# Two graph-attention layers on one core: scores, products and transposes of a tile in one run each

## The chip, the cores and the metric

The kernel runs on one core of a Trainium2 chip. The metric is device time of one execution in microseconds (us). Before the change it is 2035.97 us, the median of three runs (2034.86 to 2036.61). Differences within 0.2% (about 4 us) can't be told from no change for this kernel.

## The reference, cut to what matters

A graph of 3125 nodes with 128 features and 103,125 edges goes through a relational graph convolution with residual and normalization, and then through two attention layers with two heads of 64 features, the first followed by a relu, the second by a residual and a normalization:

```
def _transformer_conv(x, src, dst, Wq, bq, Wk, bk, Wv, bv, Ws, bs, heads):
    q = (x @ Wq + bq).reshape(n, heads, C)
    k = (x @ Wk + bk).reshape(n, heads, C)
    v = (x @ Wv + bv).reshape(n, heads, C)
    alpha = jnp.sum(q[dst] * k[src], axis=-1) / np.sqrt(C)
    amax = jax.ops.segment_max(alpha, dst, num_segments=n)
    ex = jnp.exp(alpha - amax[dst])
    denom = jax.ops.segment_sum(ex, dst, num_segments=n)
    a = ex / denom[dst]
    out = segment_sum(v[src] * a[..., None], dst).reshape(n, heads * C)
    return out + x @ Ws + bs
...
h = jax.nn.relu(_transformer_conv(x, ..., HEADS))
x = _layernorm(x + _transformer_conv(h, ..., HEADS), axis=-1)
```

All arithmetic is float32.

## The kernel before, in words

The first half of the kernel builds, among other things, a dense table `bias` of 3125 x 3125 values: the logarithm of how many edges lead from one node to another. With it the attention is done densely: for a tile of R = 125 target nodes all 3125 scores of each head are computed, the table is added, and nodes without an edge fall out in the softmax.

The function `conv` does one attention layer; it is called twice. It has T = 25 tiles. The 3125 source nodes are cut into CH = 7 chunks, six of 500 and one of 125. For a tile the work is:

- **Scores** (TensorE, L1499): for each chunk and each of the two heads one matmul of the keys `kT_l` with the queries `q_tile_l`. A head takes 64 of the 128 rows of the array, so that the two heads of a chunk can run side by side. 14 matmuls; the trace records two passes for each (float32), so 8 records are two chunks.
- **Masking** (VectorE, L1703): one operation for each chunk and head takes the scores out of their PSUM bank, adds the table and keeps the maximum. Then the row maximum is formed (L1734, L1738).
- **Exponentials** (ScalarE, L1600): four operations over a tile, two for each head.
- **Transposes** (TensorE, L1514): 50 transposes of 125x125 in 14 turns (a turn is a chunk of one head; the two short ones are turns 12 and 13). Each turn fills a PSUM bank, which ScalarE (L1608, L1610) or VectorE (L1711, turns 1, 4, 7, 10) copies to SBUF.
- **Products** (TensorE, L1485): 50 matmuls of the values with the transposed weights, each into 64 of the array's columns (two heads, two column halves); 100 records. All add up in bank `psO`.
- **Ending**: ScalarE copies the sums (L1591), TensorE transposes them and multiplies the tile by `Ws` (L1549, L1550), VectorE divides and adds (`finish`, L1654 to L1666). In layer 1 the rows are transposed once more for layer 2 (L1558, L1633). In layer 2 `center` and `normalize` (L1673 to L1685) add the residual and normalize, with a power on GpSimd (L1453) in between.

The order is written out by hand. A step t of the loop works on the scores of tile t, on the transposes and products of tile t - 1 (`u`), and on the ending of tile t - 2 (`w`). Every engine has its own `step`; counting semaphores join them. TensorE alternates: two chunks of scores, three turns, two chunks, three turns, two chunks, three turns, the short chunk, five turns, then all products. PSUM has eight banks: four hold scores (`psS`), three hold turns (`psT`), the last is `psO`.

Of the kernel before, what the change touches and what calls it, by code (L numbers as in the profile page):

```python
# [1332 lines left out]
def conv(nc, a, m, layer, out):  # L1333
# [4 lines left out]
    with ctx:  # L1338
# [3 lines left out]
        def sem(name):  # L1342
# [33 lines left out]
                 "rooted", "carried", "ot_ok", "o_ps", "x_cur", "q_laid", "kk_ps", "bq_ok")  # L1376
# [6 lines left out]
        psS, psT, psO = ps[0:4], ps[4:7], ps[7]  # L1383
        psQ = ps[4:8]
        ORDER = (0, 1, 2, 3, 4, 5, 6, 7, 8, 12, 13, 9, 10, 11)
        ON_V, ON_A = (1, 4, 7, 10), (0, 2, 3, 5, 6, 8, 12, 9, 11)
# [5 lines left out]
        def turned(u, i):  # L1392

            return u * NT + (ORDER.index(i) + 1)
# [13 lines left out]
        @block.sync  # L1408
        def _(sp):
            def step(t, par):  # L1410
                if inside(t):

                    if not is_int(t) or t >= 2:
                        sp.wait_ge(z["masked"], (t - 1) * NT)
                    sp.dma_start(bias[par][:, :], m["bias"][bass.ds(t, 1), :, :].rearrange("a p n -> (a p) n")).then_inc(b_in[par], 16)

                if layer == 2 and inside(t - 1):
                    if not is_int(t) or t >= 3:
                        sp.wait_ge(z["asked"], t - 2)
                    sp.dma_start(x_old[1 - par][:, 0, :], m["x1"][bass.ds((t - 1) * R, R), :]).then_inc(x_in[1 - par], 16)  # L1420
                if layer == 2 and inside(t - 3):
                    sp.wait_ge(z["rows_ok"], t - 2)
                    sp.dma_start(out[bass.ds((t - 3) * R, R), :], rows[1 - par][:, 0, :]).then_inc(out_ok[1 - par], 16)
            pipeline_loop(sp, step, 3)
            if layer == 2:
                sp.wait_ge(out_ok[0], 16 * ((T + 1) // 2))
                sp.wait_ge(out_ok[1], 16 * (T // 2))

        @block.gpsimd
        def _(pool):  # L1430
            nc.gpsimd.memset(half_power[:, :, :], -0.5).then_inc(z["one"], 1)
            pool.wait_ge(z["one"], 1)
            pool.wait_ge(z["q_ok"], 1)

            def lay_q(t, par):

                if not is_int(t) or t >= 2:
                    pool.wait_ge(z["qk"], (t - 1) * NT)
                nc.gpsimd.tensor_copy(q_now[par][:, :], qT[:, bass.ds(t * R, R)]).then_inc(z["q_laid"], 1)  # L1439

            lay_q(0, 0)
            pool.wait_ge(z["q_ok"], CH)

            def step(t, par):
                if inside(t + 1):
                    lay_q(t + 1, 1 - par)
                if inside(t - 2):
                    if not is_int(t) or t >= 4:
                        pool.wait_ge(z["o_ps"], t - 3)
                    nc.gpsimd.tensor_copy(x_now[par][:, :], inT[:, bass.ds((t - 2) * R, R)]).then_inc(z["x_cur"], 1)  # L1450
                if layer == 2 and inside(t - 2):
                    pool.wait_ge(z["asked"], t - 1)
                    nc.gpsimd.tensor_tensor(rstd[:, :, :], rstd[:, :, :], half_power[:, :, :], ALU.pow).then_inc(z["rooted"], 1)  # L1453
            pipeline_loop(pool, step)

        @block.tensor
        def _(pe):
# [31 lines left out]
            def scores(t, par, j):  # L1489
                if j == 0:  # L1490
                    pe.wait_ge(z["q_laid"], t + 1)
                if is_int(t) and t == 0:
                    pe.wait_ge(z["k_ok"], j + 1)

                if not is_int(t) or t * CH + j >= 2:
                    pe.wait_ge(z["masked"], (t * CH + (j - 2)) * 2 + 2)
                for hd in range(HEADS):
                    own = slice(HD * hd, HD * (hd + 1))
                    nc.tensor.matmul(psS[2 * ((par + j) % 2) + hd][0:R, 0:cw[j]], q_now[par][own, :],  # L1499
                                     kT[own, CW * j:CW * j + cw[j]], start=True, stop=True).then_inc(z["qk"], 1)  # L1500

            def turn(u, up, i):
                c, hd = i // HEADS, i % HEADS
                if c in (0, EXP_AT):
                    pe.wait_ge(z["exp_ok"], u * 4 + (hd + 1 + 2 * (c > 0)))

                if 3 <= i < 12:
                    chunk_out(pe, u, i - 3)
                elif i < 3 and (not is_int(u) or u >= 1):
                    chunk_out(pe, u - 1, i + 9)  # L1510
                for b in range(cw[c] // R):
                    n = 4 * c + b
                    to = psT[i % 3][0:R, b * R:(b + 1) * R] if c < CH - 1 else psO[0:R, 128 * (hd + 1):128 * (hd + 1) + R]
                    last = nc.tensor.transpose(to, S[up][:, hd, n * R:(n + 1) * R], eye[0:R, 0:R])  # L1514
                last.then_inc(z["t_ps"], 1)
# [18 lines left out]
            def step(t, par):  # L1534
# [7 lines left out]
                if is_int(t) and t == 1:  # L1542
                    pe.wait_ge(z["v_ok"], len(groups))
# [7 lines left out]
                if inside(t):  # L1551
                    scores(t, par, 2)
                    scores(t, par, 3)
                if inside(u):
                    turns(u, up, 3, 6)
# [3 lines left out]
                if inside(t):  # L1559
                    scores(t, par, 4)  # L1560
                    scores(t, par, 5)
                if inside(u):
                    turns(u, up, 6, 9)
                if inside(t):
                    scores(t, par, 6)
                if inside(w):
                    pe.wait_ge(z["fin_ok"] if layer == 2 else z["r_ok"], w + 1)
                if inside(u):
# [8 lines left out]
        def _(act):  # L1577
# [25 lines left out]
            def turned_out(u, i):  # L1603
# [3 lines left out]
                if c < CH - 1:  # L1607
                    nc.scalar.copy(PT[i][:, 0:cw[c]], psT[i % 3][0:R, 0:cw[c]]).then_inc(z["pa_ok"], 1)  # L1608
                else:
                    nc.scalar.copy(PT[i][:, 0:256].rearrange("p (h n) -> p h n", h=HEADS)[:, :, 0:R],  # L1610
                                   psO[0:R, 128:384].rearrange("p (h n) -> p h n", h=HEADS)[:, :, 0:R]).then_inc(z["pa_ok"], 1)

            def step(t, par):
                u, up, w = t - 1, 1 - par, t - 2
                if inside(u):
                    for i in (0, 2, 3, 5):
                        turned_out(u, i)
                if layer == 1 and inside(w):
                    rows_turned(w, par)
                if inside(u):  # L1620
                    for i in (6, 8, 12, 9, 11):
                        turned_out(u, i)
                if inside(t):
                    for n in range(3):
                        exps(t, par, n)
                if inside(u):
                    sums_out(u, up)
                if inside(t):
                    exps(t, par, 3)
# [7 lines left out]
        def _(v):  # L1637
# [49 lines left out]
            CHAIN = 2 if layer == 1 else 6  # L1687

            def step(t, par):
# [7 lines left out]
                def mask(j):  # L1697
                    v.wait_ge(z["carried"], t * CH + j) if not is_int(t) or t * CH + j > 0 else None
                    v.wait_ge(z["qk"], (t * CH + (j + 1)) * 2)
                    V.memset(spare[:, :], 0.0).then_inc(z["carried"], 1)  # L1700
                    for hd in range(HEADS):
                        lo, hi = CW * j, CW * j + cw[j]
                        V.tensor_tensor_reduce(S[par][:, hd, lo:hi], psS[2 * ((par + j) % 2) + hd][0:R, 0:cw[j]],  # L1703
# [3 lines left out]
                def turned_out(i):  # L1707
# [3 lines left out]
                    V.tensor_copy(PT[i][:, 0:cw[c]], psT[i % 3][0:R, 0:cw[c]]).then_inc(z["pt"], 1)  # L1711

                if inside(t):
                    mask(0)
                    mask(1)
                if inside(u):
                    turned_out(1)
                if inside(w):
                    finish(w, par, then)
                if inside(t):  # L1720
                    mask(2)
                    mask(3)
                if inside(u):
                    turned_out(4)
                if inside(t):
                    mask(4)
                    mask(5)
                if inside(u):
                    turned_out(7)
# [9 lines left out]
                if is_int(t) and t == 0:  # L1739
                    values_out()  # L1740
                if inside(u):
                    turned_out(10)
                if layer == 2 and inside(w):
                    center(w, par, then)
                    normalize(w, par)
            pipeline_loop(v, step)
# [21 lines left out]
```

## Time and profile before

| | |
|---|---|
| Median of three runs | 2035.97 us |
| The profiled execution | 2030.42 us, span 2028.5 us |
| TensorE matmul busy | 1952.3 us, 96% of the span |
| TensorE weight loads busy | 1633.2 us, 81% |
| VectorE busy | 1431.0 us, 71% |
| ScalarE busy | 1297.1 us, 64% |
| Mean granted TensorE clock | 0.986 |
| Attention, layer 1 (first projection to next layer's) | 1066.79 to 1547.72 us |
| Attention, layer 2 (first projection to the end) | 1547.72 to 2028.5 us |

The span is from the first to the last instruction; the time of an execution is a little more. Ends of matmuls are modelled in the trace and they overlap in the array, so what TensorE really spends on a group is read from the start of one row to the start of the next, not from the row's length. The two attention layers are about half of the time, each some 481 us, and nearly all of it is 24 like steps.

### The profile page before, as it was taken

To read this page: it belongs to the slowest core of one execution; us is meant where nothing else is said; L and a number is where in the kernel's file an instruction comes from. 1 tells how busy PE (TensorE), PEld (TensorE's weight loads), DVE (VectorE), ACT (ScalarE), POOL (GpSimd) and SP (SyncE) were. 2 spreads that over 40 slices of the span, in tenths; PEclk is the share of its full clock that TensorE was granted. 3 is DMA by queue.
4 is the path that set the end of the run, shared out by engine and by line. 5 is a ranking of instruction groups with operands and counts; after the bars stand their busy time and mean duration, and the time that the engine had idled before them with its cause. 6 is when DMAs were issued, how large, how long until landed. Compare 5 with 4: busy or idle time off the path is not lost. (4 is left out here: it accounts for less than half of the span.)

```text
span 2028.5 us, 53132 instructions
## 1 busy us (share of the span) xinstructions
PE 1952.3 (96%) x19165; PEld 1633.2 (81%) x19165; DVE 1431.0 (71%) x4127; ACT 1297.1 (64%) x2289; POOL 671.6 (33%) x802
## 2 busy tenths in 40 slices
PE   1799999999999999999989999999999999999998
PEld 1789999999999999999975777777776777777777
DVE  3888878878887887888635666666663766677665
ACT  1566766767676676767645666666664666666665
POOL 3676577566657656665210000000000000000000
PEclk8899999999999999999999999999999999999999
DMA  3012111111211111121013222222211233222220
GB/s 80 9 38 76 42 40 52 65 39 39 77 40 40 53 64 39 39 78 37 34 67 128 96 69 90 95 95 84 73 63 71 94 104 103 84 87 101 102 102 8
DMA packets 43018, 137.00 MB, mean 68 GB/s; under 512 B 9190, under 2 KB 24359, under 8 KB 36484
## 3 DMA queue, kind: packets, MB, share of 16 engines
q1 hardware_dynamic: 38484, 128.24, 17.7%
q0 software_dynamic: 4400, 6.80, 1.4%
q8 instruction: 104, 1.70, 0.4%
q14 instruction: 30, 0.25, 0.0%
HBM read 91.83 MB, written 43.20 MB: 67 GB/s over the span
## 5 line engine op out<-in xcount | busy, mean ns | idle before, releaser
L854 PE MATMUL ps<-matrixT,x_rows 125*128 125x256 f32 (+1 forms) x2500 | 563.5, 377 | 0.1
L1703 DVE CUSTOM_DVE_ANT_0 scores_l<-ps,bias_rows_l 125x500 f32<-125x500 f32 (+1 forms) x700 | 396.6, 619 | 212.5 <-issue 212.5
L854 PEld LDWEIGHTS ps<-matrixT,x_rows 125*128 125x128 f32 x2500 | 461.3, 190 | 48.4 <-issue 0.2
L1608 ACT COPY weightsT_l<-ps 125x500 f32<-125x500 f32 x400 | 230.4, 577 | 293.4 <-PE ps L1514 292.8
L945 ACT COPY matrixT<-ps 125x500 f32<-125x500 f32 (+2 forms) x800 | 381.9, 652 | 44.3 <-PE ps L842 44.3
L1514 PEld LDWEIGHTS ps<-eye,scores_l 125*125 125x125 f32 x2500 | 287.8, 188 | 114.5 <-issue 106.7
L842 PE MATMUL ps<-high_weights,low_onehot 64*125 64x125 f32 x6300 | 368.2, 275 | 11.1 <-DVE high_weights L722 11.1
L842 PEld LDWEIGHTS ps<-high_weights,low_onehot 64*125 64x125 f32 x6300 | 357.9, 189 | 24.7 <-issue 15.8
L1514 PE MATMUL ps<-eye,scores_l 125*125 125x125 f32 x2500 | 324.9, 280 | 1.3 <-ACT weightsT_l L1608 1.3
L1600 ACT ACTIVATE scores_l<-scores_l,neg_max_l 125x1500 f32<-125x1500 f32 x200 | 318.0, 1594 | 7.5 <-DVE neg_max_l L1738 7.5
L1499 PE MATMUL ps<-kT_l,q_tile_l 64*125 64x500 f32 (+1 forms) x1400 | 317.0, 564 | 1.5 <-DVE chunk_max_l L1703 1.2
L719 DVE TENSOR_TENSOR low_onehot<-own_low,digitsT 128x1000 f32<-128x1000 f32 x200 | 281.4, 1407 | 0.0
L1485 PE MATMUL ps<-weightsT_l,values_l 125*64 125x125 f32 x5000 | 279.7, 271 | 0.0
L1485 PEld LDWEIGHTS ps<-weightsT_l,values_l 125*64 125x64 f32 x5000 | 267.8, 136 | 5.9
L722 DVE TENSOR_TENSOR high_weights<-high_weights,edge_weightsT 128x800 f32<-128x800 f32 x200 | 222.7, 1114 | 0.0
L1499 PEld LDWEIGHTS ps<-kT_l,q_tile_l 64*125 64x125 f32 x1400 | 114.7, 182 | 103.9 <-issue 63.0
L574 POOL TENSOR_TENSOR coef_parts<-kinds,comp 128x512 f32<-128x512 f32 x97 | 120.2, 1239 | 231.3 <-DVE digits L690 227.4
L972 ACT ACTIVATE ln<-ps,tiny 125x1000 f32<-125x1000 bf16 x100 | 95.4, 954 | 125.8 <-DVE bias L738 85.3
L1439 POOL COPY q_tile_l<-qT_l 128x125 f32 (+1 forms) x52 | 15.2, 292 | 463.6 <-PE ps L1499 428.0
L955 ACT CAST countsT<-matrixT 125x512 bf16<-125x512 f32 (+1 forms) x200 | 162.1, 948 | 0.0
L717 DVE TENSOR_TENSOR high_weights<-iota,digitsT 128x200 f32<-128x200 f32 x200 | 79.4, 397 | 101.9 <-PE ps L842 95.1
L1453 POOL TENSOR_TENSOR rstd_l<-rstd_l,minus_half_l 125x1 f32<-125x1 f32 x25 | 13.7, 548 | 414.1 <-DVE rstd_l L1679 414.1
(152 smaller groups left out, 1725.7 us busy)
## 6 DMA issues: line engine op xcount, KB each, us to landing
bias_rows_l<-bias SPq DMA_DIRECT2D x50, 1562.5 KB, 6.7
bias<-bias SPq DMA_DIRECT2D x75, 500.0 KB
x_rows<-in_x SPq DMA_DIRECT2D x1, 1562.5 KB
bias<-bias SPq DMA_DIRECT2D x25, 62.5 KB
x<-x_rows SPq DMA_DIRECT2D x25, 62.5 KB
x_rows_l<-x SPq DMA_DIRECT2D x25, 62.5 KB
out<-rows_l SPq DMA_DIRECT2D x25, 62.5 KB
dst_int<-in_dst SPq DMA_DIRECT2D x1, 402.8 KB
```

Source lines behind the costliest of these rows:

```text
L719: V.tensor_tensor(L[:, at, 0:p, :], own_low[:, :].unsqueeze(1).to_broadcast([128, p, R]), digitsT[par][:, 0, to].unsqueeze(2).to_broadcast ...
L722: V.tensor_tensor(Hw[:, at, 0:p, 0:BASES * T].rearrange("p n (h b) -> p n h b", b=BASES), hots.unsqueeze(3).to_broadcast([128, p, T, BASES ...
L842: last = nc.tensor.matmul(psP[2 * bank + q][0:R, 128 * (i % 4):128 * (i % 4) + COLS], L[own, at, i % GROUP, :], Hw[own, at, i % GROUP, 0:C ...
L854: last = nc.tensor.matmul(psG[:, BASES * SPLIT * side:BASES * (SPLIT * side + SIDE[side])], x[:, h, :], MT[side][:, 0:SIDE[side], BASES * ...
L945: last = nc.scalar.copy(MT[side][:, at:at + 2 * c - 1:2, 0:COLS], psP[2 * (g % 3) + q][0:R, :].rearrange("p (i c) -> p i c", c=128)[:, 0:c ...
L955: nc.scalar.copy(CT[:, lo:hi, SPLIT * side:SPLIT * side + SIDE[side]], MT[side][:, 0:SIDE[side], BASES * T + lo:BASES * T + hi].rearrange( ...
L1485: last = nc.tensor.matmul(psO[HD * hd:HD * (hd + 1), 0:R], vals[:, 4 * c + b, hd, :], weights, start=(c == 0 and b == 0), stop=(c == CH - ...
L1499: nc.tensor.matmul(psS[2 * ((par + j) % 2) + hd][0:R, 0:cw[j]], q_now[par][own, :], kT[own, CW * j:CW * j + cw[j]], start=True, stop=True) ...
L1514: last = nc.tensor.transpose(to, S[up][:, hd, n * R:(n + 1) * R], eye[0:R, 0:R])
L1600: nc.scalar.activation(part, part, ACT.Exp, bias=neg[par][:, hd:hd + 1], accum_out=sums[par][:, hd, n // 2:n // 2 + 1]).then_inc(z["exp_ok ...
L1608: nc.scalar.copy(PT[i][:, 0:cw[c]], psT[i % 3][0:R, 0:cw[c]]).then_inc(z["pa_ok"], 1)
L1703: V.tensor_tensor_reduce(S[par][:, hd, lo:hi], psS[2 * ((par + j) % 2) + hd][0:R, 0:cw[j]], bias[par][0:R, lo:hi], 1.0, FLOOR, ALU.add, AL ...
```

## The change: what it does

The order within a step, the use of the PSUM banks and the tile on which each part works are changed; no arithmetic is.

- TensorE does all seven chunks of scores of tile t in one run, then all products of tile t - 2, then the transposes of tile t - 1 in one run, with the two ending matmuls still behind the first three turns. The products move one step later. In steps after the first the short chunk comes first (`chunk`).
- Seven banks form one ring `psR` for scores and turns; `psO` keeps only the sums and the ending. The two short turns share a bank of the ring. Each score matmul now has a wait of its own: for the copy that frees its bank of the last turn in it, or for the masking that frees it of an earlier score. The first turns wait for the masking.
- ScalarE does the exponentials of tile t - 1 at the start of step t (before: those of tile t at the end of step t), then the copy of the sums, then all its copies of turns, then the copy of the rows.
- VectorE masks all chunks first, then forms the maximum, then in layer 2 does `center` and `normalize` of tile t - 3 (before: of t - 2 at the end of the step), then its four copies with `finish` behind the first. GpSimd and the DMA queue follow one step later in layer 2.

TensorE's order in a step of layer 1 before (L1499 scores, L1514 transposes, L1549, L1550 and L1558 ending, L1485 products):

```order
L1499 MATMUL ps<-kT_l,q_tile_l 125x500 x4
L1514 MATMUL ps<-eye,scores_l 125x125 x12
L1549 MATMUL ps<-eye,sumsT_l 125x128
L1550 MATMUL ps<-Ws,in_tile_l 125x128
L1499 MATMUL ps<-kT_l,q_tile_l 125x500 x4
L1514 MATMUL ps<-eye,scores_l 125x125 x12
L1558 MATMUL ps<-eye,rows_l 128x125
L1499 MATMUL ps<-kT_l,q_tile_l 125x500 x4
L1514 MATMUL ps<-eye,scores_l 125x125 x12
L1499 MATMUL ps<-kT_l,q_tile_l 125x125 x2
L1514 MATMUL ps<-eye,scores_l 125x125 x14
L1485 MATMUL ps<-weightsT_l,values_l 64x125 x50
```

The same step in the changed kernel (L1522 scores, L1499 products, L1540 transposes, L1578, L1579 and L1584 ending):

```order
L1522 MATMUL ps<-kT_l,q_tile_l 125x125 x2
L1522 MATMUL ps<-kT_l,q_tile_l 125x500 x12
L1499 MATMUL ps<-weightsT_l,values_l 64x125 x50
L1540 MATMUL ps<-eye,scores_l 125x125 x12
L1578 MATMUL ps<-eye,sumsT_l 125x128
L1579 MATMUL ps<-Ws,in_tile_l 125x128
L1540 MATMUL ps<-eye,scores_l 125x125 x38
L1584 MATMUL ps<-eye,rows_l 128x125
```

The number of matmuls is the same. Four runs of scores and four of transposes have become one of each.

ScalarE's order in a step of layer 1 before (L1608 and L1610 copies of turns, L1633 copy of the rows, L1600 exponentials, L1591 copy of the sums):

```order
L1608 COPY weightsT_l<-ps 125x500 x4
L1633 COPY hT<-ps 128x125
L1608 COPY weightsT_l<-ps 125x500 x2
L1610 COPY weightsT_l<-ps 125x2x125
L1608 COPY weightsT_l<-ps 125x500 x2
L1600 ACTIVATE scores_l,part_sums_l<-scores_l,neg_max_l 125x1500 x2
L1600 ACTIVATE scores_l,part_sums_l<-scores_l,neg_max_l 125x1625
L1591 COPY sumsT_l<-ps 128x125
L1600 ACTIVATE scores_l,part_sums_l<-scores_l,neg_max_l 125x1625
```

And in the changed kernel (L1611 exponentials, L1602 sums, L1619 and L1621 turns, L1639 rows):

```order
L1611 ACTIVATE scores_l,part_sums_l<-scores_l,neg_max_l 125x1500 x2
L1611 ACTIVATE scores_l,part_sums_l<-scores_l,neg_max_l 125x1625 x2
L1602 COPY sumsT_l<-ps 128x125
L1619 COPY weightsT_l<-ps 125x500 x8
L1621 COPY weightsT_l<-ps 125x2x125
L1639 COPY hT<-ps 128x125
```

The exponentials now stand ahead of all copies of the step, and the copies follow each other.

The diff, cut to its core:

```diff
-        psS, psT, psO = ps[0:4], ps[4:7], ps[7]
-        psQ = ps[4:8]
+        psR, psO, psQ = ps[0:7], ps[7], ps[4:8]
+        RING = len(psR)
...
+        def chunk(t, n):
+            return n if is_int(t) and t == 0 else (n - 1) % CH
+        def score_bank(t, k):
+            return psR[k % 4] if is_int(t) and t == 0 else psR[k % RING]
+        def turn_bank(i):
+            return psR[min(i, NT - 2) % RING]
+        def last_turned(b):
+            return b + RING if b + RING < NT - 1 else b
... (DMA queue and GpSimd, layer 2: x1, out and the power one step later)
-                if not is_int(t) or t * CH + j >= 2:
-                    pe.wait_ge(z["masked"], (t * CH + (j - 2)) * 2 + 2)
+                if is_int(t) and t == 1 and n == 0:
+                    pe.wait_ge(z["v_ok"], len(groups))
+                    pe.wait_ge(z["masked"], NT)
                 for hd in range(HEADS):
...
+                    elif k >= RING:
+                        pe.wait_ge(z["masked"], t * NT + (k - RING + 1))
+                    elif not is_int(t) or t >= 2:
+                        chunk_out(pe, t - 2, last_turned(k))
...
-                if 3 <= i < 12:
-                    chunk_out(pe, u, i - 3)
-                elif i < 3 and (not is_int(u) or u >= 1):
-                    chunk_out(pe, u - 1, i + 9)
+                if i < RING:
+                    if inside(u + 1):
+                        pe.wait_ge(z["masked"], (u + 1) * NT + (i + RING + 1))
+                    else:
+                        chunk_out(pe, u - 1, last_turned(i))
+                elif i < NT - 1:
+                    chunk_out(pe, u, i - RING)
... (TensorE's step)
                 if inside(t):
-                    scores(t, par, 0)
-                    scores(t, par, 1)
+                    for j in range(CH):
+                        scores(t, par, j)
+                if inside(w):
+                    if not is_int(w) or w >= 1:
+                        pe.wait_ge(z["fin_ok"] if layer == 2 else z["r_ok"], w)
+                    for c in range(CH):
+                        product(w, c)
                 if inside(u):
                     turns(u, up, 0, 3)
...
                 if inside(u):
-                    turns(u, up, 3, 6)
+                    turns(u, up, 3, NT)
...
-                    turns(u, up, 12, 14)
-                    turns(u, up, 9, 12)
-                    chunk_out(pe, u, 12)
-                    for c in range(CH):
-                        product(u, c)
... (ScalarE's step)
                 if inside(u):
-                    for i in (0, 2, 3, 5):
+                    for n in range(4):
+                        exps(u, up, n)
+                if inside(w):
+                    sums_out(w, par)
+                if inside(u):
+                    for i in ON_A:
                         turned_out(u, i)
... (VectorE's step, behind the maximum)
+                if layer == 2 and inside(t - 3):
+                    center(t - 3, 1 - par, Steps(v, z["mid"], (t - 3) * 4))
+                    normalize(t - 3, 1 - par)
                 if inside(u):
+                    turned_out(1)
+                if inside(w):
+                    finish(w, par, then)
+                if inside(u):
+                    turned_out(4)
+                    turned_out(7)
                     turned_out(10)
```

## Rows read from the trace of the kernel before

**Rows 1.** The page's busy times: us, share of the span, instructions.

```profile
PE 1952.3 (96%) x19165; PEld 1633.2 (81%) x19165; DVE 1431.0 (71%) x4127; ACT 1297.1 (64%) x2289; POOL 671.6 (33%) x802
```

**Rows 2.** Who waited for whom: total us, times, longest.

```profile
PEld ps L1514 <- issue: 106.7, 144, 0.7
```

**Rows 3.** Timeline, TensorE, one step of layer 2: start, us, records.

```profile
1719.29 1.95 PE L1499 MATMUL ps<-kT_l,q_tile_l 64*125 64x500 f32 x8
1721.16 1.57 PE L1514 MATMUL ps<-eye,scores_l 125*125 125x125 f32 x12
1722.57 0.28 PE L1549 MATMUL ps<-eye,sumsT_l 128*125 128x128 f32 x1
...
1722.99 1.95 PE L1499 MATMUL ps<-kT_l,q_tile_l 64*125 64x500 f32 x8
1724.87 1.57 PE L1514 MATMUL ps<-eye,scores_l 125*125 125x125 f32 x12
1726.37 1.94 PE L1499 MATMUL ps<-kT_l,q_tile_l 64*125 64x500 f32 x8
...
1729.75 0.48 PE L1499 MATMUL ps<-kT_l,q_tile_l 64*125 64x125 f32 x4
1730.16 1.79 PE L1514 MATMUL ps<-eye,scores_l 125*125 125x125 f32 x14
1731.88 5.59 PE L1485 MATMUL ps<-weightsT_l,values_l 125*64 125x125 f32 x100
1737.41 1.11 PE L1499 MATMUL ps<-kT_l,q_tile_l 64*125 64x500 f32 x4
```

**Rows 4.** Timeline, layer 1's projections: matmuls of 500 columns on the whole array.

```profile
1074.74 1.00 PE L1465 MATMUL ps<-xT,Wq 128*128 128x500 f32 x2
1075.58 1.00 PE L1466 MATMUL ps<-xT,Wk 128*128 128x500 f32 x2
```

**Rows 5.** Timeline, all engines: scores and their masking in a step of layer 1.

```profile
1404.16 0.19 PEld L1499 LDWEIGHTS ps<-kT_l,q_tile_l 64*125 64x125 f32 x2 [0.23 <-issue]
...
1404.83 0.67 DVE L1703 CUSTOM_DVE_ANT_0 scores_l<-ps,bias_rows_l 125x500 f32<-125x500 f32 x1 [6.28 <-issue]
...
1405.43 0.68 DVE L1703 CUSTOM_DVE_ANT_0 scores_l<-ps,bias_rows_l 125x500 f32<-125x500 f32 x1
...
1411.50 0.08 DVE L1703 DVE_READ_ACCUMULATOR2_ANT chunk_max_l<- 125x1 f32 x1
...
1411.64 0.33 PEld L1499 LDWEIGHTS ps<-kT_l,q_tile_l 64*125 64x125 f32 x4 [0.51 <-DVE chunk_max_l L1703]
```

**Rows 6.** Timeline: a turn and its copy, and two copies back to back.

```profile
1423.75 1.57 PE L1514 MATMUL ps<-eye,scores_l 125*125 125x125 f32 x12
...
1424.58 0.58 ACT L1608 COPY weightsT_l<-ps 125x500 f32<-125x500 f32 x1 [0.68 <-PE ps L1514]
...
2011.18 1.04 ACT L1608 COPY weightsT_l<-ps 125x500 f32<-125x500 f32 x2
```

**Rows 7.** The page's groups: exponentials, VectorE's copies; count, busy us, mean ns.

```profile
L1600 ACT ACTIVATE scores_l<-scores_l,neg_max_l 125x1500 f32<-125x1500 f32 x200 | 318.0, 1594 | 7.5 <-DVE neg_max_l L1738 7.5
...
L1711 DVE COPY weightsT_l<-ps 125x500 f32<-125x500 f32 x200 | 135.0, 675 | 20.0 <-PE ps L1514 16.8
```

**Rows 8.** Timeline: start of step 1 of layer 1.

```profile
1093.37 0.89 DVE L1646 TENSOR_TENSOR values_l<-ps,bv 125x512 f32<-125x512 f32 x2 [0.18 <-PE ps L1475]
...
1093.48 1.95 PE L1499 MATMUL ps<-kT_l,q_tile_l 64*125 64x500 f32 x8
```

**Rows 9.** Timeline: TensorE at the end of layer 2.

```profile
2003.74 5.59 PE L1485 MATMUL ps<-weightsT_l,values_l 125*64 125x125 f32 x100
...
2009.26 1.57 PE L1514 MATMUL ps<-eye,scores_l 125*125 125x125 f32 x12
...
2011.80 4.63 PE L1514 MATMUL ps<-eye,scores_l 125*125 125x125 f32 x38 [0.64 <-ACT weightsT_l L1608]
...
2016.36 5.59 PE L1485 MATMUL ps<-weightsT_l,values_l 125*64 125x125 f32 x100
```

More of the change, by code:

```diff
@@ L1415, in step @@
                     sp.dma_start(bias[par][:, :], m["bias"][bass.ds(t, 1), :, :].rearrange("a p n -> (a p) n")).then_inc(b_in[par], 16)
[L1417 to L1424, printed above, removed]
+                if layer == 2 and inside(t - 2):
+                    if not is_int(t) or t >= 4:
+                        sp.wait_ge(z["asked"], t - 3)
+                    sp.dma_start(x_old[par][:, 0, :], m["x1"][bass.ds((t - 2) * R, R), :]).then_inc(x_in[par], 16)
+                if layer == 2 and inside(t - 4):
+                    sp.wait_ge(z["rows_ok"], t - 3)
+                    sp.dma_start(out[bass.ds((t - 4) * R, R), :], rows[par][:, 0, :]).then_inc(out_ok[par], 16)
+            pipeline_loop(sp, step, 4)
             if layer == 2:
@@ L1450, in step @@
                     nc.gpsimd.tensor_copy(x_now[par][:, :], inT[:, bass.ds((t - 2) * R, R)]).then_inc(z["x_cur"], 1)
-                if layer == 2 and inside(t - 2):
-                    pool.wait_ge(z["asked"], t - 1)
+                if layer == 2 and inside(t - 3):
+                    pool.wait_ge(z["asked"], t - 2)
                     nc.gpsimd.tensor_tensor(rstd[:, :, :], rstd[:, :, :], half_power[:, :, :], ALU.pow).then_inc(z["rooted"], 1)
-            pipeline_loop(pool, step)
+            pipeline_loop(pool, step, layer + 1)
         @block.tensor
@@ L1487, in product, with scores @@
                 last.then_inc(z["pv_ok"], 1)
-            def scores(t, par, j):
-                if j == 0:
+            def scores(t, par, n):
+                j = chunk(t, n)
+                if n == 0:
                     pe.wait_ge(z["q_laid"], t + 1)
@@ L1619, in step @@
                     rows_turned(w, par)
[L1620 to L1629, printed above, removed]
             def rows_turned(w, par):
@@ L1685, in normalize @@
                 V.tensor_scalar(r, r, mean[:, 0, 0:1], rstd[:, 0, :], ALU.subtract, ALU.mult).then_inc(z["rows_ok"], 1)
-            CHAIN = 2 if layer == 1 else 6
+            CHAIN = 2
             def step(t, par):
@@ L1696, in step, with mask @@
                         v.wait_ge(z["neg_ok"], t - 1)
-                def mask(j):
-                    v.wait_ge(z["carried"], t * CH + j) if not is_int(t) or t * CH + j > 0 else None
-                    v.wait_ge(z["qk"], (t * CH + (j + 1)) * 2)
+                def mask(n):
+                    j = chunk(t, n)
+                    v.wait_ge(z["carried"], t * CH + n) if not is_int(t) or t * CH + n > 0 else None
+                    v.wait_ge(z["qk"], (t * CH + (n + 1)) * 2)
                     V.memset(spare[:, :], 0.0).then_inc(z["carried"], 1)
@@ L1710, in turned_out @@
                     buffer_free(v, u, i)
-                    V.tensor_copy(PT[i][:, 0:cw[c]], psT[i % 3][0:R, 0:cw[c]]).then_inc(z["pt"], 1)
+                    V.tensor_copy(PT[i][:, 0:cw[c]], turn_bank(i)[0:R, 0:cw[c]]).then_inc(z["pt"], 1)
                 if inside(t):
[L1714 to L1729, printed above, removed]
+                    for j in range(CH - 1):
+                        mask(j)
                 if inside(t):
@@ L1740, in step @@
                     values_out()
+                if layer == 2 and inside(t - 3):
+                    center(t - 3, 1 - par, Steps(v, z["mid"], (t - 3) * 4))
+                    normalize(t - 3, 1 - par)
                 if inside(u):
+                    turned_out(1)
[4 more added lines that the diff above has]
+                    turned_out(7)
                     turned_out(10)
[L1743 to L1746, printed above, removed]
+            pipeline_loop(v, step, layer + 1)
 INPUTS = ['x', 'src', 'dst', 'edge_type_8', 'edge_weight', 'L0_gnn_V', 'L0_gnn_w_comp', 'L0_gnn_loop_w', 'L0_gnn_bias',
```

39 lines of the change are left out of this document (13 added, 26 removed).

## The prediction, written before the changed kernel ran

> **What bounds the kernel now.** I read the page's busy times first: TensorE is busy 96% of the span, no other compute engine above 71% [rows 1]. Next the timeline of TensorE over one step of layer 2 [rows 3]: from one run of scores to the same run a step later it is 1737.41 - 1719.29 = 18.12 us, and no row carries a wait. So TensorE sets the pace of the attention, and a reordering pays only if TensorE's own stream gets shorter. The view of waits puts 106.7 us of idle time of the weight loads ahead of the transposes down to "issue" [rows 2], that is to nothing the profile can name. I take this as the clue and look at what a change of kind costs in the stream.
>
> **What a change of kind costs.** Five turns (14 transposes) take 1731.88 - 1730.16 = 1.72 us and three turns (12) take 1726.37 - 1724.87 = 1.50 [rows 3]; two transposes are 0.22 us, one 0.11. Twelve of them are 1.31 us, so a run of transposes between two runs of another kind has 0.19 to 0.20 us that belongs to no transpose. The run that is followed by the ending, also on the whole array, takes 1722.57 - 1721.16 = 1.41 [rows 3]: about 0.10 of it lies at the entry, 0.09 at the exit. Scores: a matmul of 500 columns on the whole array takes 1075.58 - 1074.74 = 0.84 us [rows 4], and two heads side by side should take the same; two chunks are then 1.68, and the row shows 1721.16 - 1719.29 = 1.87: again 0.20 for entry and exit. The short chunk: 1730.16 - 1729.75 = 0.41, of which two passes like a transpose's are 0.21 and 0.20 the change. The products take 5.52 us with scores behind them [rows 3] and 2009.26 - 2003.74 = 5.52 with transposes behind them [rows 9], so what follows them does not matter.
>
> The Trainium skill ("TensorEngine Tiling (Array Packing)", Key Properties) says that changing the tiling mode, not just the tile, drains TensorE. By that rule, the trace agrees (transposes and the ending, both on the whole array, follow each other at 0.11 us, and the extra 0.20 us stands where whole-array work meets the 64-row halves of the scores), the new change from scores to products would be paid too, as I count it below.
>
> **The step after the change, part by part.** Scores: 0.20 + 0.21 + 6 x 0.84 = 5.45 us in place of 3 x 1.87 + 0.41 = 6.03. Transposes: 0.20 + 50 x 0.109 = 5.65 in place of 1.41 + 1.50 + 1.50 + 1.72 = 6.13 plus the exit of 0.09 that stands behind the ending. Products: 5.52 both times. Ending: 0.33 (1722.99 - 1722.57 less the exit). The sum is 16.95 us against 18.12: **1.17 us less a step**. The one change of kind that the trace never shows is scores to products. Its bounds: nothing extra at all (-0.15 against what I have counted) and a double price (+0.20); I take the same 0.1 to exit as everywhere, since it is what every exit shown costs.
>
> **What of the rest could be late.** Times below are from the start of a run of transposes (X) or of scores (Y).
> - Ring, transposes to scores. Turn 10 ends at X + 0.10 + 11 x 0.436 + 0.33 = 5.23. A copy starts 0.29 us behind the end of a turn (turn 0 ends at 1423.75 + 0.10 + 0.44, its copy starts at 1424.58 [rows 6]) and VectorE's takes 0.68 [rows 7]: bank free at 6.20. Scores begin at X + 5.98, and the fourth score matmul, the one in that bank, at 6.30 with its weights wanted 0.1 earlier: late by 0 to 0.1. ScalarE's last copies: turn 11 ends at 5.67, copy from 5.96; two copies back to back take 1.04 [rows 6], so 0.46 apart, the short one starts at 6.42 and frees its bank near 6.8; the sixth score matmul wants it at 7.0. It fits, by 0.2 us.
> - Ring, scores to scores. VectorE masks a score of 500 in 1405.43 - 1404.83 = 0.60 us, TensorE makes one in 0.42, so VectorE falls behind and the ring of seven must take it up. The first long mask starts 0.67 us behind the start of its second pass (1404.83 - 1404.16 [rows 5]): Y + 0.32 + 0.42 + 0.67 = 1.41. The seventh mask, which frees the bank of the last score, starts 4 x 0.60 later and ends 0.68 after that, at 4.49. A waiting weight load starts 0.06 after the mask's end (1411.64 against 1411.58 [rows 5]) and needs 0.1. The last score is due at Y + 0.32 + 5 x 0.84 = 4.51 and comes at 4.65: **late by 0.14 us**, and its second pass may again lose the 0.1 of an entry. No earlier score is late. I take 0.17 us a step; bounds 0 and 0.35, the upper one with turn 10's copy late too.
> - Exponentials. Four take 4 x 1.594 = 6.4 us [rows 7] and start at about Y + 0.9, behind the last copy; the transposes need the first two at Y + 5.45 + 5.52 = 11.0. Hidden by 3 us and more.
> - VectorE. Masks end near Y + 8.7; the maximum, and in layer 2 the centering of the tile before, fit ahead of turn 1 at Y + 12.1. Behind turn 1 it has `finish` and three copies in the 4 us to the end of the run, which is why turn 10 is the tight one. The queue of DMAs runs more than a step ahead; x1, the table and the output move by a step, none onto the path.
> - Products. They wait for copies made a step earlier, nothing is queued behind a copy any more there.
>
> **Start and end of each layer.** Step 1 of a layer may not begin its scores before the last values are copied, since the ring has taken over their banks: 1093.37 + 0.89 = 1094.26 in place of 1093.48 [rows 8], with reaction 0.9 us later, in each layer: +1.8. At the end the last turns stand alone: 2016.36 - 2009.26 = 7.10 us before, with a wait of 0.64 for a copy [rows 9]. Now 5.65 + 0.33, and some 0.4 for the sums, which ScalarE copies only behind the exponentials: 6.4, so -0.7 in each. In layer 1 the last products wait for the copy of the rows that was just asked for: +1.0. Together +1.4.
>
> **The sum.** 24 steps of each layer save 1.17 and lose 0.17: 48 x 1.00 = 48.0 us less, 1.4 more: -46.6. The profiled execution took 2030.42 us, so it would be 1983.8. It lies 5.5 us under the median of the runs, and I carry the difference over: 2035.97 - 46.6 = **1989 us**, 2.3% faster.
>
> **The rivals.**
> - *Nothing is late* (0.10). The masks keep up a little better, or the transition to the products is free: 48 x 1.17 and more, 54 to 60 us less: 1979. For it: the slack missed is 0.14 us. Against it: 0.60 against 0.42 us is from rows.
> - *The ring stalls more* (0.20). A stall costs its lateness and, as at a change of kind, the 0.1 of a restart; two or three of them in a step (turn 10's copy, turn 11's, the last scores) cost 0.3 to 0.8 us. Saved: 17 to 40 us, middle 2007. For it: all of these margins are under 0.2 us. Against it: a late score delays the turns behind it too, so the copies gain what TensorE loses.
> - *The heads part* (0.06), slower. Every score matmul now has a wait of its own; before only the first of a pair had one. If the second head's wait holds it until the first head's pass is under way or done, the pair loses its overlap. It decides from 1.17 / 7 = 0.17 us a pair; fully serial it is 6 x 0.84 + 0.2 = 5.2 us a step, 48 x 4.0 more than now: 2230. Against it: waits between like matmuls cost nothing in the runs of transposes, one for each four.
> - *Scores at VectorE's pace* (0.04), slower. If banks come free so late that the run goes at 0.60 instead of 0.42 us from its first score, it costs 12 x 0.18 = 2.2 us a step against the 1.17 saved: +49 us, 2085. Decides from 1.17 us of stalls. The Trainium skill ("TensorEngine Tiling (Array Packing)", PSUM Bottleneck) speaks for it: tiling speeds up TensorE but not the evacuation of PSUM. Against it: only the last of 14 meets a bank not yet free.
> - *The change does not remove what it seems to* (0.04). The 0.2 us belong to the semaphore waits at these places, which stay, and not to the change of kind; then within 4 us of before. Against it: the second pair in each run of scores has such a wait too and starts on time.
>
> **How the numbers follow.** My forecast has 0.56 and spans 1983 to 1998; with the rivals beside it the range of 1978 to 2008 leaves out the slower cases, the case of no change and the worst of the stalls, 0.2 together. Faster by over 0.2%: 0.56 + 0.10 + 0.20 = 0.86. Within 0.2%, which is about what a measurement can't tell from nothing: 0.04. Slower: 0.10.
>
> **What would show it.** TensorE's timeline of a step has three runs, 16.95 to 17.2 us from one run of scores to the next in layer 2 and 0.11 more in layer 1. The scores last 5.45 to 5.7, the only wait within them is the last one's, on a mask. The products still take 5.52, the transposes with the ending 5.98. The idle time of weight loads ahead of the transposes put down to "issue" falls by more than half. Wrong would be: runs of scores near 7 us or more (pace of the masks, or parted heads), a wait ahead of turn 0 for an exponential, or three runs of unchanged total length.

## The result and the profile after

The changed kernel takes 1991.47 us (median of four runs, 1990.22 to 1992.74); the kernel before, measured beside it, 2036.29. The ratio is 0.9773, 95% interval 0.9760 to 0.9786: 2.3% faster. The forecast was 1989 us, within a range of 1978 to 2008. In the text below, a kind of work is scores, products or whole-array work (transposes and the ending), and a change of kind is the place where one follows another.

One step of layer 2 on TensorE, from the timeline of the changed kernel (start, us, engine, line, operation, records), answers to [rows 3]:

```profile
1708.84 5.67 PE L1522 MATMUL ps<-kT_l,q_tile_l 64*125 64x125 f32 x28
1714.43 5.59 PE L1499 MATMUL ps<-weightsT_l,values_l 125*64 125x125 f32 x100
1719.96 1.57 PE L1540 MATMUL ps<-eye,scores_l 125*125 125x125 f32 x12
1721.37 0.28 PE L1578 MATMUL ps<-eye,sumsT_l 128*125 128x128 f32 x1
...
1721.70 4.31 PE L1540 MATMUL ps<-eye,scores_l 125*125 125x125 f32 x38
1725.94 0.95 PE L1522 MATMUL ps<-kT_l,q_tile_l 64*125 64x125 f32 x6
```

Three runs, none with a wait ahead of it. From one run of scores to the next it is 17.10 us where it was 18.12. The same matmuls are done; what went is the time around them. By starts:

| A step of layer 2, us | before | forecast | after |
|---|---|---|---|
| scores | 6.04 | 5.45 + 0.17 | 5.59 |
| products | 5.53 | 5.52 | 5.53 |
| transposes and ending | 6.55 | 5.98 | 5.98 |
| whole step | 18.12 | 17.12 | 17.10 |

The page's busy times (us, share, instructions) answer to [rows 1]:

```profile
PE 1911.6 (96%) x19165; PEld 1655.2 (83%) x19165; DVE 1450.3 (73%) x4127; ACT 1282.1 (64%) x2289; POOL 670.9 (34%) x802
```

TensorE is as busy as before, 96%, though its stream is 2% shorter: the share of busy time does not see the time between kinds, for the rows overlap (1708.84 + 5.67 is 1714.51, and the next row starts at 1714.43). The view of waits answers to [rows 2] (106.7 us before):

```profile
PEld ps L1499 <- issue: 34.1, 46, 0.7
...
PEld ps L1522 <- DVE chunk_max_l L1710: 12.7, 60, 0.2
...
PEld ps L1540 <- issue: 9.6, 51, 0.7
```

The idle time of the transposes' weight loads put down to "issue" has gone from 106.7 to 9.6 us. That is not the gain: 0.74 us of such idle time stood ahead of the transposes 144 times, three to a step, each behind a long chunk of scores. It now stands ahead of the products 46 times, once a step, 34.1 us. The view marks most of the changes of kind and prices none: a change costs about 0.2 us of the stream, also where this line shows no idle time. The line on the masks does not price the ring's late bank either: its 0.2 us each is what a weight load within the run of scores shows also where nothing is late. The late bank is seen in the timeline of all engines in the step before the one shown:

```profile
1691.73 5.67 PE L1522 MATMUL ps<-kT_l,q_tile_l 64*125 64x125 f32 x28
...
1693.15 0.67 DVE L1710 CUSTOM_DVE_ANT_0 scores_l<-ps,bias_rows_l 125x500 f32<-125x500 f32 x1 [0.26 <-issue]
...
1696.16 0.09 DVE L1710 DVE_READ_ACCUMULATOR2_ANT chunk_max_l<- 125x1 f32 x1
1696.24 0.34 PEld L1522 LDWEIGHTS ps<-kT_l,q_tile_l 64*125 64x125 f32 x3 [0.23 <-issue]
...
1697.33 5.60 PE L1499 MATMUL ps<-weightsT_l,values_l 125*64 125x125 f32 x100
```

The first long mask starts 1.42 us into the run (the walk said 1.41) and the seventh ends at 1696.25, 4.52 into it (4.49). The last three weight loads, the last score's among them, take from 1696.24 to 1696.58, and the run lasts 5.60 us in place of the 5.45 of the sum without a late score.

### The profile page after: what moved, and what is told of

Read it like the earlier page. It is cut to its first block and busy times, and to the rows that moved or that the text cites. A ratio compares the mean times of both kernels' runs of the same rounds, so it can differ in the third digit from the quotient of the medians.

```text
span 1989.5 us, 53432 instructions
## 1 busy us (share of the span) xinstructions
PE 1911.6 (96%) x19165; PEld 1655.2 (83%) x19165; DVE 1450.3 (73%) x4127; ACT 1282.1 (64%) x2289; POOL 670.9 (34%) x802
## 5 line engine op out<-in xcount | busy, mean ns | idle before, releaser
L1710 DVE CUSTOM_DVE_ANT_0 scores_l<-ps,bias_rows_l 125x500 f32<-125x500 f32 (+1 forms) x700 | 390.0, 619 | 25.7 <-issue 24.9
L842 PE MATMUL ps<-high_weights,low_onehot 64*125 64x125 f32 x6300 | 377.6, 276 | 12.5 <-DVE high_weights L722 11.1
L842 PEld LDWEIGHTS ps<-high_weights,low_onehot 64*125 64x125 f32 x6300 | 362.2, 189 | 31.2 <-issue 17.9
L1611 ACT ACTIVATE scores_l<-scores_l,neg_max_l 125x1500 f32<-125x1500 f32 x200 | 317.3, 1600 | 7.3 <-DVE neg_max_l L1731 7.3
L1499 PEld LDWEIGHTS ps<-weightsT_l,values_l 125*64 125x64 f32 x5000 | 267.9, 136 | 36.4 <-issue 34.1
L1540 PE MATMUL ps<-eye,scores_l 125*125 125x125 f32 x2500 | 295.2, 275 | 0.0
L1540 PEld LDWEIGHTS ps<-eye,scores_l 125*125 125x125 f32 x2500 | 281.2, 189 | 10.1 <-issue 9.6
L1522 PE MATMUL ps<-kT_l,q_tile_l 64*125 64x500 f32 (+1 forms) x1400 | 286.9, 547 | 1.7 <-issue 1.6
L1499 PE MATMUL ps<-weightsT_l,values_l 125*64 125x125 f32 x5000 | 279.7, 270 | 1.6 <-ACT hT L1639 1.6
L1619 ACT COPY weightsT_l<-ps 125x500 f32<-125x500 f32 x400 | 220.4, 577 | 93.0 <-PE ps L1540 88.1
L1718 DVE COPY weightsT_l<-ps 125x500 f32<-125x500 f32 x200 | 135.1, 677 | 158.4 <-PE ps L1540 158.1
L1522 PEld LDWEIGHTS ps<-kT_l,q_tile_l 64*125 64x125 f32 x1400 | 143.9, 183 | 112.2 <-issue 77.7
```

What stands on the lines that cost most here:

```text
L842: last = nc.tensor.matmul(psP[2 * bank + q][0:R, 128 * (i % 4):128 * (i % 4) + COLS], L[own, at, i % GROUP, :], Hw[own, at, i % GROUP, 0:C ...
L1499: last = nc.tensor.matmul(psO[HD * hd:HD * (hd + 1), 0:R], vals[:, 4 * c + b, hd, :], weights, start=(c == 0 and b == 0), stop=(c == CH - ...
L1522: nc.tensor.matmul(score_bank(t, k)[0:R, 0:cw[j]], q_now[par][own, :], kT[own, CW * j:CW * j + cw[j]], start=True, stop=True).then_inc(z[" ...
L1540: last = nc.tensor.transpose(turn_bank(i)[0:R, at:at + R], S[up][:, hd, n * R:(n + 1) * R], eye[0:R, 0:R])
L1611: nc.scalar.activation(part, part, ACT.Exp, bias=neg[par][:, hd:hd + 1], accum_out=sums[par][:, hd, n // 2:n // 2 + 1]).then_inc(z["exp_ok ...
L1619: nc.scalar.copy(PT[i][:, 0:cw[c]], turn_bank(i)[0:R, 0:cw[c]]).then_inc(z["pa_ok"], 1)
```

## The experiments

In each, theory and rival are those on record. Ratios are to the kernel before, run on the same chip in the same job. Where kernels ran in different jobs I compare the attention stage of their traces, from the first projection of layer 1 to the end of the span (961.7 us before, 911.8 after), for a reason that the first two runs show.

**Both kernels once more.** No edit.

> The kernel before, unchanged, once more. The attention stage lasts 961.7 us in its first trace. Theory 1: the first half of the program (all ahead of the attention, 1066.8 us in that trace and 1077.7 us in the changed kernel's, on the same code) differs from execution to execution, so here it may be anything from 1066 to 1078 us. Theory 2: it belongs to the program; here it is 1066.8 us again.

> The changed kernel, unchanged, once more. Attention stage 911.8 us. Theory 1 (the first half varies by execution): 1066 to 1078 us. Theory 2 (it belongs to the program, of which the change moved something): 1077.7 us again. The clock at the seam of the two layers: full speed again if it belongs to the program, half for 7 us as in the kernel before if it is by chance.

Measured: 2029.43 us (ratio of the copy to the kernel before 1.001) and 1979.82 us (0.9769, 0.9753 to 0.9785). The stage ahead of the attention took 1066.9 us in both. It took 1064 to 1067 us in all four traces of this job, on four different kernels, and 1077 to 1080 us in the four of the next job. The third job, on the chip of the same number as the first, shows 1076.6 and 1077.6, and the medians of the kernel before are 2027.58, 2038.11 and 2039.67 us in the three jobs. So in these traces it goes neither with the kernel nor with the single execution but with the job: theory 2 falls, and theory 1 is right that it varies and wrong on what with. Its code is the same in every kernel here. What in a job sets it was not tested; in the first pair of traces 9.4 of the 10.9 us show as more busy time of the matmuls of L842.

The attention stage took 957.9 us in the repeated kernel before and again 911.8 in the changed one. Of the 3.8 us between the two traces of before, 3.0 are the clock at the seam of the layers and 0.8 stand in the first projections of layer 1, where the half level also lasted longer in the first trace. The first projections of layer 2 in the first trace of before:

```profile
1547.72 2.04 PE L1465 MATMUL ps<-hT,Wq 128*128 128x500 f32 x2 [0.99 <-POOL minus_half_l L1431]
1549.55 1.87 PE L1466 MATMUL ps<-hT,Wk 128*128 128x500 f32 x2
```

and in the repeated one:

```profile
1546.98 1.10 PE L1465 MATMUL ps<-hT,Wq 128*128 128x500 f32 x2 [0.99 <-POOL minus_half_l L1431]
1547.93 1.00 PE L1466 MATMUL ps<-hT,Wk 128*128 128x500 f32 x2
```

The same two passes take 1.83 us at a granted clock of 0.50 (1.2 GHz) and 0.95 at 1.00 (2.4 GHz), after the same idle time of TensorE (0.99 us). Seven microseconds at half level were seen once in two traces of the kernel before. The changed kernel ran at full level here in two of its three traces, and in the third (the last run below) the slow clock at the seam cost 1.7 us. So it varies between executions of one kernel and is not an effect of the change.

**A change of kind, once more and twice more.** The runs of scores and products are cut:

```diff
-                if inside(t):
-                    for j in range(CH):
-                        scores(t, par, j)
-                if inside(w):
...
-                    for c in range(CH):
-                        product(w, c)
+                for lo, hi, plo, phi in ((0, 4, 0, 3), (4, 7, 3, 7)):
+                    if inside(t):
+                        for j in range(lo, hi):
+                            scores(t, par, j)
+                    if inside(w):
...
+                        for c in range(plo, phi):
+                            product(w, c)
```

(twice: `(0, 3, 0, 2), (3, 5, 2, 4), (5, 7, 4, 7)`)

> The changed kernel with the scores and the products of a step cut once: four chunks of scores, three of products, three of scores, four of products. It adds one change from scores to products and one from products to scores, no wait. Theory A (a change of kind costs 0.15 to 0.20 us whatever stands there): 0.35 us more a step, less at most 0.13 since the late score at the end of a run is no longer late: 46 steps x 0.22 to 0.35, 10 to 16 us over the changed kernel. Theory B (the gaps belonged to the semaphore waits at these places and the gain has another source): no change, within 3 us.

> The same, cut twice (3, 2 and 2 chunks of scores between 2, 2 and 3 of products): two changes of kind more again. Theory A: a further 16 us, 26 to 32 us over the changed kernel. Theory B: no change.

Measured: 1989.70 us (0.9821, 0.9804 to 0.9837), 9.9 us over the changed kernel of the same job, and 2008.26 us (0.9907, 0.9891 to 0.9924), 28.4 over. TensorE's timeline with one cut:

```profile
1719.93 3.05 PE L1522 MATMUL ps<-kT_l,q_tile_l 64*125 64x125 f32 x16
1722.91 2.80 PE L1499 MATMUL ps<-weightsT_l,values_l 125*64 125x125 f32 x48
1725.64 2.78 PE L1522 MATMUL ps<-kT_l,q_tile_l 64*125 64x500 f32 x12
1728.36 3.01 PE L1499 MATMUL ps<-weightsT_l,values_l 125*64 125x125 f32 x52
1731.30 0.37 PE L1540 MATMUL ps<-eye,scores_l 125*125 125x125 f32 x1
```

The same scores and products take 11.37 us in four runs and 11.12 in two (1708.84 to 1719.96 above), 0.25 us more. The late score is on time now, which gives back 0.14; and the 0.05 us by which turn 10's copy is late in layer 2 is no longer hidden behind it (the first four chunks take 2.98 us there and 2.93 in layer 1). That leaves 0.34 to 0.35 for the pair of changes. With the second cut nothing is left to win back and the step grows by a further 0.35 us (18.6 us over 46 steps is 0.40; the trace shows 17.70 against 17.35). Both medians bear out theory A, the first at the lower edge of its range (10 to 16 us) and the second within it (26 to 32). Theory B falls: no wait was added, and the time went up. What came back is a pair between scores and products, at 0.35 to 0.40 us, where the three pairs that the change took out lay between scores and transposes, read from the trace of before at 0.39 each. The last kind was not put back by itself. Only the pair is measured, not scores to products alone.

**The order without the ring.**

```diff
-            return psR[k % 4] if is_int(t) and t == 0 else psR[k % RING]
+            return psR[k % 4]
...
-            return psR[min(i, NT - 2) % RING]
+            return psR[4 + min(i, NT - 2) % 3]
```

(and the waits to match: for the mask four scores back, for the copy three turns back)

> The new order alone: three runs a step, but over the banks of the kernel before, four for scores and three for turns. If the ring is needed (a bank is free for a score only when the mask four scores back is done, 0.60 us each and both heads of a chunk at once): scores 2.1 us longer a step than the 5.6 of the changed kernel; turns wait for the copy three turns back (0.436 + 0.29 + 0.58 + 0.16 = 1.47 us for what takes 1.31), and for turn 4's copy behind the division: 1.0 us. A step of 20.2 us, 48 x 3.1 = 149 us over the changed kernel, ratio to the kernel before 1.05. If TensorE's saving does not hang on the ring: ratio 0.977 as for the changed kernel.

Measured: 2126.60 us, ratio 1.0428 (1.0410 to 1.0445). The new order alone makes the kernel 4% slower. The attention stage is 134 us longer than the changed kernel's (149 expected). TensorE waits for a mask ahead of each score:

```profile
1766.01 7.53 PE L1520 MATMUL ps<-kT_l,q_tile_l 64*125 64x125 f32 x28
...
1768.75 0.29 PEld L1520 LDWEIGHTS ps<-kT_l,q_tile_l 64*125 64x125 f32 x2 [0.31 <-DVE chunk_max_l L1706]
...
1769.36 0.29 PEld L1520 LDWEIGHTS ps<-kT_l,q_tile_l 64*125 64x125 f32 x2 [0.32 <-DVE chunk_max_l L1706]
...
1773.47 1.73 PE L1499 MATMUL ps<-weightsT_l,values_l 125*64 125x125 f32 x28
```

One score each 0.60 us or a little more, the pace of the masks, and 7.46 us for the run (the expectation said 7.7). That is 1.87 us more a step; the rest, 0.8 to 1.0 us a step, is in the transposes, which now wait for the copy three turns back. The Trainium skill's sentence ("TensorEngine Tiling (Array Packing)", PSUM Bottleneck) that tiling speeds up TensorE but not the evacuation is borne out here: two heads side by side make a score each 0.42 us, and VectorE empties one each 0.60. In the changed kernel the seven banks hold it off for all scores but the last.

**Six banks for seven.**

```diff
-        RING = len(psR)
+        RING = 6
```

(`last_turned` and the turns' wait for a mask take the last user of a bank)

> The changed kernel with a ring of six banks. Theory (late banks are priced by the same walk that gave 0.14 us for seven): the first score waits for the last short copy, 0.9 to 1.0 us; the last score waits for the eighth mask, 5.25 against 4.51 us, 0.6 us more than with seven. 1.5 us a step, 72 us more, ratio 1.01, so that the whole gain is gone. Rival (one bank less is absorbed, as seven left slack): under 10 us more.

Measured: 2065.72 us, 1.0132 (1.0115 to 1.0149); attention stage 986.4 us, 74.6 over (72 expected).

```profile
1756.64 4.31 PE L1540 MATMUL ps<-eye,scores_l 125*125 125x125 f32 x38
1761.74 6.25 PE L1522 MATMUL ps<-kT_l,q_tile_l 64*125 64x125 f32 x28 [0.79 <-ACT weightsT_l L1621]
1767.93 5.59 PE L1499 MATMUL ps<-weightsT_l,values_l 125*64 125x125 f32 x100
```

The wait for the last short copy (0.79 us) and the longer scores (6.19 us, 0.60 more) are both there, and the rival falls. One bank less turns a gain of 2.3% into a loss of 1.3%.

**The short chunk last.**

```diff
-            return n if is_int(t) and t == 0 else (n - 1) % CH
+            return n
```

> The changed kernel with the short chunk last again. Theory: the chain of masks starts earlier (1.19 in place of 1.41 us) but seven long masks stand ahead of the last score's bank; it is due at 5.14 and comes at 5.64; scores 0.3 us longer a step, 15 us more. Rival (the order of the chunks only moves the same waits): within 3 us.

Measured: 2012.37 us, 0.9872 (0.9855 to 0.9888); attention stage 931.6 us, 19.8 over (15 expected), of which about 2 are the slow clock at the starts of the two layers. The timeline:

```profile
1759.19 6.02 PE L1522 MATMUL ps<-kT_l,q_tile_l 64*125 64x500 f32 x28
...
1764.12 0.38 PEld L1522 LDWEIGHTS ps<-kT_l,q_tile_l 64*125 64x125 f32 x2 [0.31 <-DVE chunk_max_l L1710]
...
1764.73 0.29 PEld L1522 LDWEIGHTS ps<-kT_l,q_tile_l 64*125 64x125 f32 x2 [0.22 <-DVE chunk_max_l L1710]
```

Scores last 5.95 us, 0.36 more (0.3 expected): each of the two short scores meets a late mask. The line that puts the short chunk first is worth 18 us.

**The second layer's normalization in the same tile's step.**

```diff
-                if layer == 2 and inside(t - 3):
-                    center(t - 3, 1 - par, Steps(v, z["mid"], (t - 3) * 4))
-                    normalize(t - 3, 1 - par)
...
                     turned_out(10)
+                if layer == 2 and inside(w):
+                    center(w, par, then)
+                    normalize(w, par)
```

(the DMA queue and GpSimd as before the change)

> The changed kernel with the second layer's residual and normalization in the step of the division again, at the end of VectorE's step. Theory: 2.0 us of them (and a power on GpSimd in between) stand between turn 10's copy and the first mask, so masks start 1.7 us later and the ring runs out: scores 1.35 us longer in each of 23 steps of layer 2, 31 us more, nothing in layer 1. Rival (VectorE has enough idle time to absorb it): within 3 us.

Measured: 2027.07 us, 0.9943 (0.9926 to 0.9959). Layer 1's attention takes 457.8 us (457.4 in the changed kernel), layer 2's 488.7 (454.4): 34 us, all in layer 2 (31 expected). VectorE in a step:

```profile
1756.92 0.68 DVE L1718 COPY weightsT_l<-ps 125x500 f32<-125x500 f32 x1 [0.63 <-PE ps L1540]
1757.51 0.28 DVE L1679 TENSOR_TENSOR rows_l<-rows_l,x_rows_l 125x128 f32<-125x128 f32 x1
...
1759.20 0.35 DVE L1691 TENSOR_SCALAR rows_l<-rows_l,mean_l,rstd_l 125x128 f32<-125x128 f32 x1 [0.67 <-POOL rstd_l L1467]
...
1759.78 0.29 DVE L1710 CUSTOM_DVE_ANT_0 scores_l<-ps,bias_rows_l 125x125 f32<-125x125 f32 x1
```

The run of scores began at 1757.38; its first mask starts 2.4 us later, where it is 0.6 in the changed kernel, and the run lasts 7.01 us (7.45 in every other step). VectorE has idle time enough in a step, but not at this place.

**The ends of the layers.** Step 1 waits bank by bank for the values; in the last step but one the sums are copied ahead of the last exponential, and the rows are transposed between turns 8 and 9:

```diff
-                    pe.wait_ge(z["v_ok"], len(groups))
...
+                    elif is_int(t) and t == 1:
+                        if k >= 4:
+                            pe.wait_ge(z["v_ok"], k + 1)
```

> The changed kernel with the waits at the ends of a layer taken away: in step 1 each of the ring's banks 4 to 6 waits only for the values that lie in it (the first version: for all values, 1.0 us in each layer); in the last step but one ScalarE copies the sums ahead of the last exponential (0.4 us in each layer), and in layer 1 the rows are transposed between turns 8 and 9 and copied ahead of the last copies, so that the last products don't wait (0.85 us). Theory: 3.5 us less than the changed kernel, ratio to it 0.998. Rival (the ends hide them, something else is as late): within 1 us.

> The changed kernel beside the run before it, for the difference: ratio to the kernel before 0.977, attention stage 911.8 us or, with the slow clock at the seam of the layers, up to 3.5 us more.

Measured: 1989.07 us (0.9760, 0.9742 to 0.9778) and 1991.47 us (0.9767, 0.9749 to 0.9785), in one job. The medians differ by 2.4 us, but the intervals overlap, so by time alone this is not shown. The traces show the waits gone: from the start of the last transposes of layer 1 to the last products it is 1523.16 - 1517.08 = 6.08 us, against 1525.97 - 1519.04 = 6.93 in the changed kernel.

```profile
1519.04 1.57 PE L1540 MATMUL ps<-eye,scores_l 125*125 125x125 f32 x12
...
1525.97 5.59 PE L1499 MATMUL ps<-weightsT_l,values_l 125*64 125x125 f32 x100 [0.78 <-ACT hT L1639]
```

(changed kernel, with the wait for the rows' copy), and without it:

```profile
1517.08 1.57 PE L1542 MATMUL ps<-eye,scores_l 125*125 125x125 f32 x12
...
1523.16 5.59 PE L1499 MATMUL ps<-weightsT_l,values_l 125*64 125x125 f32 x100
```

Step 1 starts its scores 0.86 us earlier in each layer. Clear of the slow clock at the seam (1.5 us) the attention stage is 908.8 us against 911.8, 3.0 of the 3.5 expected; layer 1's last turns had no wait for the sums to take away. The traces bear out the theory, the medians alone do not. The remaining 7 us or so of late last scores stay.

## Why the prediction was right, step by step

The mechanism was right, and most terms of the sum held. That the forecast in microseconds came within 2.5 us owes something to luck: with the same two kernels the changed one took 1979.82 us in another job, 9 us from the forecast. What the prediction stands on is the difference.

- **The bound.** TensorE's own stream, with no wait in it. Right: every experiment that lengthened a run of TensorE lengthened the kernel by about as much, times the steps.
- **The price of a change of kind**, 0.20 us read from differences of starts. Right for the sum: the runs last what it gave, and a pair of changes added back costs 0.35 to 0.40. The unseen one, from scores to products, was taken at the price of the others. With 0.20 for the way back it costs 0.15 to 0.20, and the bounds (free, or double) are excluded. Some readings are off by 0.01 us (scores 6.03 for 6.04, products 5.52 for 5.53 in [rows 3], 4.51 for 4.52), which changes nothing.
- **The late last score**, 0.14 us and up to 0.1 for a restart, taken at 0.17. Measured 0.14 to 0.15: 5.59 us where 5.45 was the sum without it. The steps at the start of each layer have 5.72, and their timeline shows why:

```profile
1134.01 5.79 PE L1522 MATMUL ps<-kT_l,q_tile_l 64*125 64x125 f32 x28
...
1135.55 0.68 DVE L1710 CUSTOM_DVE_ANT_0 scores_l<-ps,bias_rows_l 125x500 f32<-125x500 f32 x1
```

  The first long mask starts 1.54 us into the run in place of 1.42, and so the seventh ends 4.63 into it and not 4.52. What makes the masks late there stays open. Turn 10's copy, forecast 0 to 0.1 late, delays the second head by 0.05 us in layer 2, which then disappears behind the late last score.
- **Exponentials, VectorE's ending, copies, DMAs** hidden: but for that 0.05 us, TensorE does not wait for them in a full step.
- **Starts and ends.** The late start of step 1: the run of values takes 6.53 us in place of 5.65, 0.88 (0.9 forecast). End of layer 2: 6.47 us (6.4). Last products of layer 1: 0.85 late (1.0). The products one step earlier wait as well, 0.85 us for the copy of the rows (at 1513.51 in the changed kernel's trace), which the forecast left out; against it layer 1's last turns do not wait for the sums, for which it had 0.4.
- **The sum.** -46.6 us forecast. The first pair of traces gives -49.9 in the attention stage, of which 3.4 is the slow clock of the trace of before (3.0 at the seam, 0.4 at the start of layer 1); the repeated pair gives 911.8 - 957.9 = -46.1. The two medians differ by 44.8, 47.8 and 48.2 us in the three jobs.
- **What I had not seen** is the base: I carried over a difference of 5.5 us between one trace and the runs and did not ask where it came from. The stage ahead of the attention differs by some 11 us from job to job. The forecast in microseconds hangs on the job, the one as a difference does not.
- **The rivals.** "Nothing is late" fell: the run lasts 5.59 us and not 5.45, while the split run, where no score is late, takes 2.93 + 2.72 = 5.65 in layer 1, which is 5.45 and the 0.20 of one more entry and exit. "The ring stalls more" fell at seven banks but is what six show. "The heads part" did not happen: each score has a wait of its own, and the run has no more in it than the late last score. "The change does not remove what it seems to" fell with the gain and with the split runs. "Scores at VectorE's pace" is real and needs only fewer banks.

## What to carry to other kernels

Read TensorE's time from start to start, not from its busy share: a kernel at 96% lost 1.2 us of 18 to changes between whole-array work and halves of it, and here the gain is the number of changes taken out times the price of one, less what comes late. Long runs of one kind move the pressure to PSUM, so count banks by a walk along the run (when does the engine that empties free each bank, when is it wanted) before merging; here seven pay and six lose. Work of the emptying engine that has slack over a step may still stand at the one place where the run needs it.

## What the runs showed of the hardware that I had not expected

- Work on 64-row halves followed by work on 64-column halves costs about as much as the other changes of kind: 0.35 us for the way there and back by the trace (0.40 by the medians), where scores to transposes and back is 0.39.
- A late bank costs TensorE its lateness and 0.13 to 0.15 us more: the run is 0.14 us longer for a bank freed 0.01 us after its matmul was due (4.52 against 4.51), and 0.27 for one freed 0.12 late. That fits the 0.06 of reaction and the 0.1 of a weight load that the prediction added. The two heads can run 0.05 us out of step at no cost while a later wait covers it.
- The clock at the seam of the layers was at half (granted 0.50) for 3 to 7 us in some traces and not in others of the same kernel, worth up to 3.0 us.
